# Unread identity products in TensorE's waits, LayerNorm numbers computed a stage ahead, and the gate weights quantised in the first stage

## The chip, the cores and the metric

One core of one Trainium2 chip. A core has TensorE (PE, matrix products, results in PSUM), VectorE (DVE), ScalarE (ACT), GpSimd (POOL) and SyncE (SP, which here only issues transfers). Each engine works through its own list of instructions in order and waits on semaphores for the others. The metric is the device time of one execution in microseconds, the median of three runs.

## The reference, cut to what matters

Four pairs of attention and feed-forward, each on a LayerNorm of a running x of 16 sequences x 128 tokens x 256 features, and each added to x.

```python
x = x + xattn0(_layernorm(x), ctx, ctx)   # autocorrelation by rfft/irfft, top 4 lags
x = x + ffn0(_layernorm(x), w_gate, w_up, w_down)
x = x + xattn1(_layernorm(x), ctx, ctx)   # 16 heads, window of 64
x = x + ffn1(_layernorm(x), slot_embeds, w1, b1, w2, b2)
x = x + xattn2(_layernorm(x), ctx, ctx)   # full attention
x = x + ffn2(_layernorm(x), W_r, W_k, W_v, mu_r, mu_k)
x = x + xattn3(_layernorm(x), ctx, ctx)   # rotary attention
x = x + ffn3(_layernorm(x), W1, b1, W2, b2, Wr, br)   # 8 experts, the best 2 of each token

def ffn0(x, w_gate, w_up, w_down):          # 4-bit weights in blocks of 32, 16-bit activations
    x = act_qdq(x)                          # scale: the maximum over the whole tensor
    up = act_qdq(x @ lpbq_dequant(w_up).T)
    gate = act_qdq(x @ lpbq_dequant(w_gate).T)
    sig = fixed_qdq_u16(jax.nn.sigmoid(gate))
    gate = act_qdq(gate * sig)
    return act_qdq(gate * up) @ lpbq_dequant(w_down).T

def ffn1(x, norm_gamma, slot_norm_gamma, slot_embeds, w1, b1, w2, b2):
    xn, sn = rmsnorm(x, norm_gamma), rmsnorm(slot_embeds, slot_norm_gamma)
    logits = jnp.einsum('bnd,esd->bnes', xn, sn)
    dispatch = jax.nn.softmax(logits, axis=1)
    combine = jax.nn.softmax(logits.reshape(b, n, e * s), axis=-1)
    slots = jnp.einsum('bnd,bnes->besd', xn, dispatch)
    h = jax.nn.gelu(jnp.einsum('besd,edh->besh', slots, w1) + b1)
    eo = (jnp.einsum('besh,ehd->besd', h, w2) + b2).reshape(b, e * s, DIM)
    return jnp.einsum('bmd,bnm->bnd', eo, combine)

def ffn2(x, W_r, W_k, W_v, mu_r, mu_k):     # x_prev: x of the token before
    xr, xk = mu_r * x + (1 - mu_r) * x_prev, mu_k * x + (1 - mu_k) * x_prev
    return sigmoid(xr @ W_r.T) * (square(relu(xk @ W_k.T)) @ W_v.T)
```

## The kernel before

The running x lies in SBUF for the whole program as X[:, n], 16 tiles of 128 tokens x 256 features (B = 16 tiles, G4 = 4 groups of four), and beside it `stats`, the sums that `batch_stats` (L89) takes of each tile once it has been added to. The eight stages run one after the other as functions of their own: autocorrelation (tiles and semaphores named ac_), quantised FFN (qf_), windowed attention (at_), slot FFN (sl_), full attention (at_ again), receptance FFN (rf_), rotary attention (at_), routed FFN (mo_). In the trace they begin at about 0, 122, 327, 498, 1394, 1554, 1623 and 1813 us. Each has a list of instructions for each engine, written out in its order by hand; there is no planner. At a stage's end `Tiles.clear` (L74 to 76) frees the semaphores and makes all engines meet at a barrier. `Early` holds the little that is loaded across it: the identity, the first group's context, the next key weights.

LayerNorm: `layernorm_begin` (L98) turns `stats` of all 16 tiles into mean and 1/sqrt(variance) with 16 aggregates (L102) and a chain of steps on 16 numbers per partition, each waiting for the one before (L104 to 111: add epsilon, an integer first guess, three Newton steps). It stands first in DVE's list in every stage but the first, which does it in two parts (`layernorm_part`, L135); the slot FFN has it written out. Then DVE normalises tile by tile, PE turns each tile with the identity into PSUM, and ACT or DVE copies it out.

Quantised FFN (`quantised_ffn`, L1231): DVE makes the numbers, normalises x tile by tile and takes each tile's maximum (L1544, L1548), with the quantising of the gate weights put in after tile 7 (L1517 to 1525: block maxima, scale, reciprocal, times inverse, rounding, times scale). After the last maximum it makes the scale of the whole tensor, rounds x (L1576), splits it in two halves (L1581), and PE's first hidden products follow (L1386). GATE's results are evicted, rounded by ACT (L1448), put through the sigmoid (L1453), whose table ACT loads just before the first, rounded by POOL (L1333, L1335) and multiplied on DVE (L1591). The UP products are evicted between these. The output products (L1395) wait for `prod_made`.

Attention (`attention`, L507): PE projects keys (L619), values (L653) and queries of each group of four tiles, turns x (L660), in the rotary kind also multiplies by a half-swap matrix (L646, `swap_halves`). Then a loop over the 16 sequences makes maxima (score products L687), their transpose (L694), the scores against keys (L707), the shift (L718) and the weighed values (L730) in a staggered order, and DVE and ACT follow one step behind.

Slot FFN (`slot_ffn`, L2137): 24 rows (8 of x, 8 of the slots, 8 of x) are split by DVE in two f16 halves and turned by PE (`turn_row`, L2264) in one list; then 32 steps of hidden and result products. Receptance FFN (L1026): per group a turn (L1073), products (L1081, L1087) and values (L1096). Routed FFN (L1690): logits of each tile (L1840, L1846) once br has landed, a chain on DVE that picks experts and places rows, gathers by POOL (L1967), and 23 tiles of hidden (L1889) and output products (L1900).

## Time and profile before

| | us |
|---|---|
| median of three runs (2156.86, 2160.91, 2163.70) | 2160.91 |
| profiled execution | 2156.95 |
| its span | 2154.8 |
| PE busy | 1865.7 (87%) |
| DVE busy | 1478.9 (69%) |
| ACT busy | 1116.7 (52%) |
| POOL busy | 157.5 (7%) |
| mean granted clock of TensorE | 0.928 |

A granted clock of 1.00 is 2.4 GHz, one of 0.50 is 1.2 GHz. Busy shares are means over stages with different limits: the slot FFN's 896 us and the routed FFN's 341 us are nearly all PE; the openings are not. The 2.1 us between the span and the execution's time lie around it.

### The profile page before, as it was taken

Reading aid. Unit: us, or ns where it says so; the run is one execution under the profiler, and the core shown is the slowest. Engines: PE = TensorE matmul, PEld = TensorE weight load, DVE = VectorE, ACT = ScalarE, POOL = GpSimd, SP = SyncE. Lnnn points to the kernel's source line nnn. Section 1 sums busy time; section 2 is a strip of 40 time slices with the busy share of each in tenths; the row PEclk is TensorE's granted clock in tenths of the full one; section 3 lists DMA queues with packets and bytes.
Section 4 is the critical chain, followed back from the end, with each engine's and each line's share of the span. In section 5 each row is a group of like instructions: output and inputs, shape, how many; then the busy total and the mean of one; then the engine's idle time right before and its main releaser. Section 6 shows DMA issues by size and latency. Waiting matters only on the chain. (4 is left out here: it accounts for less than half of the span.)

```text
span 2154.8 us, 40850 instructions
## 1 busy us (share of the span) xinstructions
PE 1865.7 (87%) x16258; PEld 1345.9 (62%) x16258; DVE 1478.9 (69%) x3056; ACT 1116.7 (52%) x1888; POOL 157.5 (7%) x122
## 2 busy tenths in 40 slices
PE   7949269894799999999999999889787797499995
PEld 7924145673377666677777666556564476398884
DVE  6677874556777777777777776836556565688886
ACT  3425753445356566665666565344441454367772
POOL 0001300001000000000000000000000000135441
PEclk9969689996999999999999999999988898599998
DMA  4010001002100000000000000000001000477775
GB/s 143 1 50 1 0 1 50 2 2 90 40 21 21 21 27 34 21 21 21 21 20 21 2 1 1 22 29 2 22 0 53 1 2 26 152 238 251 248 249 184
DMA packets 79451, 113.68 MB, mean 53 GB/s; under 512 B 9696, under 2 KB 62624, under 8 KB 79136
## 3 DMA queue, kind: packets, MB, share of 16 engines
q1 hardware_dynamic: 74848, 99.01, 14.1%
q0 software_dynamic: 4416, 12.06, 1.5%
q8 instruction: 131, 2.15, 0.4%
q14 instruction: 56, 0.46, 0.1%
HBM read 100.83 MB, written 10.22 MB: 52 GB/s over the span
## 5 line engine op out<-in xcount | busy, mean ns | idle before, releaser
L2344 PE MATMUL sl_ps_eo<-sl_w,sl_hT 128*128 128x256 f16 x3072 | 353.2, 273 | 0.8 <-DVE sl_hT L2582 0.7
L2321 PE MATMUL sl_ps_h<-sl_slot_inT,sl_w 128*128 128x512 f16 x1536 | 338.7, 380 | 0.5 <-ACT sl_h L2458 0.5
L2344 PEld LDWEIGHTS sl_ps_eo<-sl_w,sl_hT 128*128 128x128 f16 x3072 | 298.4, 98 | 35.9 <-DVE sl_hT L2582 1.3
L2458 ACT ACTIVATE sl_h<-sl_ps_h,sl_b1T 128x512 f32<-128x512 f32 x256 | 175.7, 687 | 170.0 <-PE sl_ps_h L2321 162.9
L2321 PEld LDWEIGHTS sl_ps_h<-sl_slot_inT,sl_w 128*128 128x128 f16 x1536 | 150.4, 98 | 176.3 <-issue 1.4
L2582 DVE TENSOR_TENSOR sl_hT<-sl_h,sl_hT 128x512 f16<-128x512 f32 x256 | 177.0, 692 | 102.1 <-ACT sl_hT L2461 97.8
L950 DVE TENSOR_REDUCE at_neg_max<-at_ps 128x8 bf16<-128x1024 f32 x96 | 117.0, 1221 | 144.2 <-PE at_ps L687 144.2
L1889 PE MATMUL mo_ps_h<-mo_xgT,mo_w 128*128 128x256 f16 x1104 | 128.0, 277 | 5.4 <-issue 4.2
L1900 PE MATMUL mo_ps_eo<-mo_w,mo_hT 128*128 128x256 f16 x1104 | 124.1, 273 | 0.0
L1889 PEld LDWEIGHTS mo_ps_h<-mo_xgT,mo_w 128*128 128x128 f16 x1104 | 109.5, 100 | 20.9 <-issue 6.6
L2593 DVE SCALAR_TENSOR_TENSOR sl_result<-sl_ps_eo,sl_b 128x256 f32<-128x256 f32 x128 | 54.3, 424 | 97.6 <-PE sl_ps_eo L2344 93.3
L1900 PEld LDWEIGHTS mo_ps_eo<-mo_w,mo_hT 128*128 128x128 f16 x1104 | 107.2, 98 | 12.0
L845 ACT ACTIVATE at_probT<-at_ps 128x1024 f32<-128x1024 f32 x96 | 98.6, 1027 | 25.5 <-PE at_ps L718 25.5
L1949 ACT ACTIVATE mo_h<-mo_ps_h,mo_b 128x256 f32<-128x256 f32 x184 | 77.0, 475 | 54.0 <-issue 46.6
L1008 POOL MEMSET at_v<- 128x2048 f32 x6 | 10.7, 1817 | 1150.5 <-POOLq L76 1150.5
L852 ACT ACTIVATE at_attT<-at_ps 128x256 f32<-128x256 f32 x48 | 18.4, 383 | 140.5 <-PE at_ps L744 140.5
L1967 POOL DMA_INDIRECT mo_xg<-x_rows,mo_from_i x46 | 66.2, 1440 | 247.7 <-DVE mo_from_i L2057 233.5
L2461 ACT ACTIVATE sl_hT<-sl_h 128x512 f16<-128x512 f32 x128 | 80.6, 629 | 4.0
L1395 PE MATMUL qf_ps_out<-qf_w_outT,qf_prodT 128*128 128x256 f16 x288 | 34.1, 279 | 49.2 <-DVE qf_prodT L1608 46.1
L1386 PE MATMUL qf_ps<-qf_xqT,qf_w_inT 128*128 128x512 f16 x288 | 66.9, 393 | 9.8 <-DVE qf_xqT L1581 6.7
L2437 ACT ACTIVATE sl_combT<-sl_ps_lt 128x512 f32<-128x512 f32 x32 | 19.1, 597 | 108.4 <-PE sl_ps_lt L2300 108.4
L2075 DVE SCALAR_TENSOR_TENSOR mo_w<-mo_w_raw,mo_w 128x1024 f16<-128x1024 f32 x46 | 56.2, 1223 | 17.4 <-issue 9.0
(385 smaller groups left out, 3631.1 us busy)
## 6 DMA issues: line engine op xcount, KB each, us to landing
mo_w_raw<-in_L_ffn_W SPq DMA_DIRECT2D x46, 1024.0 KB, 7.4
sl_w_in<-in_L_ffn_w SPq DMA_DIRECT2D x16, 1024.0 KB, 5.3
at_ctxT<-ctxT SPq DMA_DIRECT2D x9, 512.0 KB, 6.9
mo_w_raw<-pair_rows SPq DMA_DIRECT2D x4, 1024.0 KB, 9.0
mo_b<-in_L_ffn_b SPq DMA_DIRECT2D x23, 128.0 KB
at_wT<-L_attention_w SPq DMA_DIRECT2D x9, 256.0 KB, 7.0
ac_ctx_all<-in_ctx SPq DMA_DIRECT2D x4, 512.0 KB, 7.3
x_rows<-mo_xrow SPq DMA_DIRECT2D x4, 512.0 KB, 2.9
```

Of the source, the lines that this page charges most:

```text
L845: act.activation(probT[:, n % 2, 2 * pair:2 * pair + 2].rearrange("p r j q -> p r (j q)"), ps[:, at:at + 2], ACT.Exp, scale=SCALE).then_in ...
L950: dve.tensor_reduce(neg_max[:, 2 * pair:2 * pair + 2, 0:HR], ps[:, at:at + 2].rearrange("p r (j k) -> p r j k", j=HR), AX.X, ALU.max, nega ...
L1386: last = pe.matmul(pair(q)[:, g], w_inT[:, w, i, k, c * P:(c + 1) * P], xqT[:, x, k, tokens], start=(k, a) == (0, 0), stop=(k, a) == (C - ...
L1889: last = pe.matmul(ps_h[:, q % 3, j % 2], w1_of(m, wp)[:, k, j * P:(j + 1) * P], xgT[:, m % 2, xp, k], start=(k, a) == (0, 0), stop=(k, a) ...
L1900: last = pe.matmul(ps_eo[:, s, 0:D], hT[:, m % 2, hp, j, s * P:(s + 1) * P], w2_of(m, wp)[:, j], start=(j, a) == (0, 0), stop=(j, a) == (H ...
L1949: act.activation(h[:, q % 2, j % 2], ps_h[:, q % 3, j % 2], ACT.Relu, bias=b1[:, m % WB, j:j + 1], scale=1.0 / W_SCALE).then_inc(h_ready, 1)
L1967: pool.indirect_dma_start(xg[:, m % XB, s], None, env.x_rows, bass.IndirectOffsetOnAxis(ap=from_i[:, q:q + 1].bitcast(U32), axis=0)).then_ ...
L2321: last = pe.matmul(ps_h[:, j % 2], w1[:, e % 2, w, k, j * P:(j + 1) * P], slot_inT[:, q % 2, x, k].rearrange("p b s -> p (b s)"), start=(k ...
L2344: last = pe.matmul(ps_eo[:, b % 2, 0:D], hT[:, hp, j, b * P:(b + 1) * P], w2[:, e % 2, w, j], start=(j, a) == (0, 0), stop=(j, a) == (HJ - ...
L2458: act.activation(h[:, j % 2], ps_h[:, j % 2], ACT.Gelu, bias=b1T[:, q // G4, j:j + 1], scale=1.0 / W_SCALE).then_inc(h_ready, 1)
L2461: act.activation(hT[:, 0, j], h[:, j % 2], ACT.Copy).then_inc(h_high, 1)
L2582: dve.tensor_tensor(hT[:, 1, j], h[:, j % 2], hT[:, 0, j], ALU.subtract).then_inc(h_split, 1)
```

## The change

`hold_clock` multiplies the identity by itself into a PSUM bank that nothing reads at that time, so many times. It is called in PE's list at these places: quantised FFN, 18 after the sixth product has been made and before the outputs, 3 at the end; every attention, 3 (rotary: 10) before the last two queries are waited for (rotary: the last plain ones), 4 before the scores of steps 0 and 1, 2 in step 1, 3 at the end, and in the rotary kind 3 in each of the four groups between the swap and the values; slot FFN, 8 first, one before each row from m = 4, 12 at the end; receptance FFN, 5 first, 8 after turn(1), 10 before the last values, 8 at the end; routed FFN, 6 before turn_x(0), 16 before turn(0), 8 before hidden(1).

The mean and the 1/sqrt of tiles 0 to 11 for the quantised, slot, receptance and routed FFN are computed near the end of the stage before (`normal_ahead`, once `stats` of 12 tiles are restated); tiles 12 to 15 follow in the stage itself (`normal_rest`). The results lie in tiles that outlive the stages (`env.ahead`). The attentions keep `layernorm_begin`.

The gate weights are loaded in the first stage, behind wo on SP's queue and ahead of the context of groups 1 to 3, and quantised in place in four pieces by DVE after pairs 2 to 5. In the quantised FFN x is rounded and split in two halves of two groups, a spare sigmoid of one column stands before the wait for x, the first two UP evictions come after the second sigmoid, and five instead of four UP roundings come before the silus.

```diff
+def hold_clock(pe, env, bank, count):
+
+    ident = env.early.ident
+    for _ in range(count):
+        pe.matmul(bank, ident[:], ident[:], start=True, stop=True)
...
+AHEAD = 12
+
+
+def normal_ahead(dve, t, env, nth, stats_known, value, rows_only=False):
+
+    env.ahead.rows_only = rows_only
+    dve.wait_ge(stats_known, value)
+    layernorm_part(dve, t, env.ahead, nth, 0, AHEAD)
+
+
+def normal_rest(dve, t, env):
+
+    layernorm_part(dve, t, env.ahead, 0, AHEAD, B)
...
             load_weight(wo, "wo", wo_in)
+            env.gate_weights.load(sp)
             for g in range(1, G4):
...
+                if 2 <= j < 6:
+                    env.gate_weights.quantise(dve, j - 2)
+            normal_ahead(dve, t, env, 2, restated, AHEAD)
             add_pair(NPAIRS - 1)
...
                 if rotary:
                     swap_halves(C * g)
+                    enough(pe, xT_ready, 4 * g - 1)
+                    hold_clock(pe, env, ps[:, 6, 0:P], 3)
...
+            if rotary:
+                pe.wait_ge(plain_ready, 2 * JOBS - 1)
+            else:
+                pe.wait_ge(proj_out, 2 * JOBS - C)
+            hold_clock(pe, env, ps[:, 0, 0:P], 10 if rotary else 3)
             pe.wait_ge(proj_out, 2 * JOBS)
             pe.wait_ge(w_in[WO], 16)
             for n in range(B + 3):
                 if n < B:
                     turn_maxima(n)
+                if n == 1:
+                    hold_clock(pe, env, ps[:, 6, 0:P], 2)
...
                     output(n - 3)
+                if n < 2:
+                    hold_clock(pe, env, ps[:, 6, 0:P], 4)
...
+            hold_clock(pe, env, ps[:, 0, 0:P], 3)
...
+                if n == AHEAD + 3:
+                    normal_ahead(dve, t, env, 1, restated, AHEAD, rows_only=windowed)
                 if n >= 3:
                     restate(n - 3)
...
+            hold_clock(pe, env, ps_r[:, 0, 0:P], 5)
             turn(0)
             turn(1)
+            hold_clock(pe, env, ps_r[:, 0, 0:P], 8)
             pe.wait_ge(weights_in, 48)
...
+            hold_clock(pe, env, ps_x[:, 0, 0], 10)
             value(G4 - 1)
+            hold_clock(pe, env, ps_x[:, 0, 0], 8)
...
+            normal_group(0)
             dve.memset(xT[:, :, :, :, 0:1], 0.0).then_inc(zeroed, 1)
-            layernorm_begin(dve, t)
-            normal_group(0)
...
             mix(1)
+            normal_rest(dve, t, env)
             key(0)
...
-UP_OUT = (((0,), (1,)), ((2,), (3,)), ((4, 5), ()), ((6, 7), ()), ((8, 9), ()), ((10, 11), ()))
+UP_OUT = (((), (0, 1)), ((2,), (3,)), ((4, 5), ()), ((6, 7), ()), ((8, 9), ()), ((10, 11), ()))
...
+            pe.wait_ge(prod_made, FC)
+            hold_clock(pe, env, ps[:, 0, 0:P], 18)
             for n in range(B):
                 output(n)
+            hold_clock(pe, env, ps[:, 0, 0:P], 3)
...
+            act.activation(spare_sig[:], constant[:, 1:2], ACT.Sigmoid).then_inc(table_loaded, 1)
             act.wait_ge(x_ready, G4)
...
-            layernorm_begin(dve, t)
             for n in range(B):
                 normal_x(n)
...
-                if n == 7:
-                    for piece in range(4):
-                        quantise_weights(0, piece)
-                if n == 11:
-                    weights_low(0)
+                if n == AHEAD - 1:
+                    weights_low_tile(0)
+                    weights_low_tile(1)
+                    normal_rest(dve, t, env)
+                    weights_low_tile(2)
...
-            for g in range(G4):
-                round_x(g)
-            for g in range(G4):
-                low_x(g)
+            for half in range(2):
+                for g in (2 * half, 2 * half + 1):
+                    round_x(g)
+                for g in (2 * half, 2 * half + 1):
+                    low_x(g)
...
+            hold_clock(pe, env, ps_h[:, 0, 0, 0:P], 6)
             turn_x(0)
...
             pe.wait_ge(table_ready, 1)
+            hold_clock(pe, env, ps_h[:, 0, 0, 0:P], 16)
             turn(0)
             for m in range(NTILES):
+                if m == 1:
+                    hold_clock(pe, env, ps_eo[:, 0, 0:P], 8)
                 hidden(m)
...
-            layernorm_begin(dve, t)
             for n in range(B):
+                if n == AHEAD:
+                    normal_rest(dve, t, env)
...
+            hold_clock(pe, env, ps_eo[:, 1, 0:P], 8)
             pe.wait_ge(consts_in, CONSTS)
...
             for m in range(NT):
+                if m >= 4:
+                    hold_clock(pe, env, ps_eo[:, 1, 0:P], 1)
                 turn_row(m)
...
             combine(STEPS - 1, 3)
+            hold_clock(pe, env, ps_h[:, 0, 0:P], 12)
...
+                if m == FIRST_SLOT + E + AHEAD - B // 2 - 2:
+                    normal_rest(dve, t, env)
                 if FIRST_SLOT <= m < NT - 2:
                     row(m + 2)
```

## Rows read from the trace of the kernel before

**Rows 1.** Line of the page: TensorE's granted clock in tenths, 40 slices
```profile
PEclk9969689996999999999999999999988898599998
```

**Rows 2.** The table of stretches: us, each engine's busy time, granted clock, DMA share, GB/s
```profile
1812.80:1874.20 61.40, 28.74 (x174) 26.32 (x175) 36.45 (x157) 15.61 (x39) 8.60 (x8) 0.50 0.47 148
...
600.00:1390.00 790.00, 786.63 (x5976) 550.28 (x5974) 575.35 (x1164) 470.00 (x848) 0.00 (x0) 1.00 0.05 17
```

**Rows 3.** The same table, PE alone: two runs of one-tile f32 products
```profile
9.96:13.51 3.55, 3.55 (x16) 1.00 1.11 355
...
18.45:20.23 1.78, 1.78 (x17) 1.00 1.07 369
```

**Rows 4.** Timeline (start, us, engine, line, tiles, [idle before <- releaser]): DVE, first stage
```profile
48.45 0.87 DVE L436 MAX8 ac_top<-ac_corr 128x8 f32<-128x128 f32 x4 [2.03 <-ACT ac_corr L378]
...
120.08 0.69 DVE L463 TENSOR_TENSOR X<-X,ac_ps_out 128x512 f32<-128x512 f32 x1 [6.52 <-PE ac_ps_out L324]
```

**Rows 5.** Timeline, DVE and PE, opening of the quantised FFN
```profile
122.88 1.17 DVE L102 BATCH_NORM_AGGREGATE qf_meanvar<-stats 128x2 f32<-128x6 f32 x16
...
126.60 0.73 DVE L1544 TENSOR_SCALAR qf_xn_ring<-X,qf_meanvar,qf_rstd 128x256 f32<-128x256 f32 x2
...
131.47 1.74 DVE L1517 TENSOR_REDUCE qf_wmax<-qf_upT 128x48 f32<-128x1536 f32 x1
...
136.75 1.76 DVE L1525 TENSOR_TENSOR qf_upT<-qf_upT,qf_wscale 128x1536 f32<-128x1536 f32 x1
...
153.98 5.25 PE L1386 MATMUL qf_ps<-qf_xqT,qf_w_inT 128*128 128x512 f16 x16 [6.67 <-DVE qf_xqT L1581]
```

**Rows 6.** Timeline, ACT, the first sigmoid
```profile
200.18 1.28 ACT L1453 ACT_TABLE_LOAD   x1
```

**Rows 7.** Timeline, PE, output products of the quantised FFN
```profile
287.55 5.50 PE L1395 MATMUL qf_ps_out<-qf_w_outT,qf_prodT 128*128 128x256 f16 x36 [46.10 <-DVE qf_prodT L1608]
...
293.50 4.09 PE L1395 MATMUL qf_ps_out<-qf_w_outT,qf_prodT 128*128 128x256 f16 x36 [0.45 <-DVE stats L91]
```

**Rows 8.** Timeline, POOL, opening of the slot FFN
```profile
507.04 4.61 POOL L2509 MEMSET sl_acc<- 128x4112 f32 x1 [8.22 <-ACT sl_acc L2414]
```

**Rows 9.** Timeline, PE, first keys of the full attention
```profile
1394.66 6.21 PE L619 MATMUL at_ps<-early_ctxT,early_wk 128*128 128x512 f32 x8 [5.01 <-PEq L76]
...
1400.70 3.60 PE L619 MATMUL at_ps<-at_ctxT,early_wk 128*128 128x512 f32 x8
```

**Rows 10.** Timeline, PE, first steps of the full attention
```profile
1454.56 2.09 PE L687 MATMUL at_ps<-at_KT,at_QT 32*128 32x128 f32 x32 [0.99 <-ACT at_probT L845]
...
1462.01 1.17 PE L687 MATMUL at_ps<-at_KT,at_QT 32*128 32x128 f32 x32
```

**Rows 11.** Timeline, DVE and PE, receptance FFN
```profile
1563.75 2.74 DVE L1161 SCALAR_TENSOR_TENSOR rf_mixedT<-rf_xT,rf_mu_rest,rf_now 128x512 f32<-128x512 f32 x4 [3.30 <-ACT rf_now L1122]
...
1565.31 6.22 PE L1081 MATMUL rf_ps_r<-rf_wT,rf_mixedT 128*128 128x256 f32 x16 [0.96 <-DVE rf_mixedT L1161]
...
1604.12 3.62 PE L1096 MATMUL rf_ps_v<-rf_wT,rf_keyT 128*128 128x256 f32 x16
...
1612.23 6.66 PE L1096 MATMUL rf_ps_v<-rf_wT,rf_keyT 128*128 128x256 f32 x16 [4.49 <-DVE rf_keyT L1169]
```

**Rows 12.** Timeline, DVE and PE, rotary attention
```profile
1647.04 0.69 DVE L924 TENSOR_TENSOR at_by_sin<-at_ps,at_sinT 128x512 f32<-128x512 f32 x1 [0.57 <-PE at_ps L646]
...
1706.36 0.29 PE L694 MATMUL at_ps<-at_ident_b,at_neg_max 128*128 128x128 bf16 x1 [4.42 <-ACT at_QT L825]
```

**Rows 13.** Timeline, PE, routed FFN's opening
```profile
1818.74 1.11 PE L1840 MATMUL mo_ps_t<-mo_ident,mo_xn_all 128*128 128x128 f32 x4 [7.59 <-DMA mo_br<-in_L_ffn_br]
...
1836.48 1.72 PE L1846 MATMUL mo_ps_m<-mo_wr,mo_xT 128*128 128x8 f32 x8
...
1869.92 7.49 PE L1889 MATMUL mo_ps_h<-mo_xgT,mo_w 128*128 128x256 f16 x48 [1.21 <-ACT mo_xgT L1926]
...
1880.96 7.07 PE L1889 MATMUL mo_ps_h<-mo_xgT,mo_w 128*128 128x256 f16 x48 [3.11 <-issue]
```

More of the change, by code:

```diff
@@ L1271, in quantised_ffn @@
         spare = upT[:].rearrange("p c n -> p (c n)").rearrange("p (s n) -> p s n", n=FF * C)
[L1272 removed]
+        raw, raw_t = [spare[:, 0], env.gate_weights.raw[:], spare[:, 6]], [spare[:, 2], None, spare[:, 7]]
         x_ints = xT[:].bitcast(I16).rearrange("p c (n half) -> p c n half", half=2)[:, :, :, 0]
@@ L1494, in _ @@
                     weights_high_tile((6, 8)[c])
-            for c in range(4):
+            for c in range(UP_FIRST):
                 round_up(c)
@@ L2720, in __init__ @@
         self.x_rows, self.pair_rows = scratch
-        self.early = None
+        self.early = self.ahead = self.gate_weights = None
+class Ahead:
+    def __init__(self, nc, ctx):
+        self.meanvar = ctx.enter_context(nc.sbuf_tensor("ahead_meanvar", [P, B, 2], F32))
+        self.rstd = ctx.enter_context(nc.sbuf_tensor("ahead_rstd", [P, B, 1], F32))
+        self.rows_only = False
 class Early:
@@ L2762, in build_program @@
         env.early = Early(nc, ctx, env)
-        for phase in PHASES:
+        env.ahead = Ahead(nc, ctx)
+        with ExitStack() as first:
+            env.gate_weights = GateWeights(nc, first, env)
+            for phase in PHASES[:2]:
+                phase(nc, env)
+        for phase in PHASES[2:]:
             phase(nc, env)
```

146 lines of the change are left out of this document (83 added, 63 removed).

## The prediction, made before the changed kernel was run

> **What bounds the kernel now.** I read the page's table of busy shares and its line of granted clock first [rows 1]. TensorE is busy for 87% of the span, but the clock line has digits under 9: there the engine runs at 1.2 GHz instead of 2.4. The table of stretches shows both kinds of time [rows 2]: from 600 to 1390 us (the slot FFN's steps) PE is busy 786.63 of 790 us at full clock, and nothing the change does can shorten that. From 1812.8 to 1874.2 it is busy 28.74 of 61.4 us at a granted clock of 0.50, while it waits for others. The same view, laid over every digit under 9, gives half-clock stretches of some 310 us in all, all at openings, ends and first steps of stages; much of them is idle PE, where the clock costs nothing.
>
> Each stage closes with a barrier of all engines (L74 to 76), so a microsecond gained in a stage's opening moves everything behind it. The sum is therefore made stage by stage: for each edit I ask what the last wait of that stretch was. The chain of waits only shows the last stage, so I used the timelines of the stretches around the edits.
>
> **The price of a hold.** One hold is one 128x128 f32 product. The forward transforms of the first stage have this form: eight of them (16 records) take 3.55 us at the slow pace and 1.78 us, with a 17th record at the edge, at the fast one [rows 3]; the clock column says 1.00 for both, as it has no record yet for the first, so it is the pace that tells them apart. So a hold is about 0.43 us at half clock and 0.222 us at full. The change issues 189 of them: 84 us if all stood on the path at the slow price, 0 if all fall into waits.
>
> **Part 1: first stage (autocorrelation).** The load of w_gate goes onto SP's queue ahead of the context of groups 1 to 3. Its 786 KB delay them by an estimated 2 to 4 us, and the second group's context is there 9 us before PE first wants it: nothing. The four pieces of quantising it (6.95 us in all, in rows 5 from 131.47 to 138.42, pieces of 2.49, 1.79, 1.00 and 1.67) go to DVE after pair j = 2 to 5; DVE waits 2.03 us for the correlation ahead of its top-values step [rows 4]. Only the first piece is longer, by 0.46, and PE has more slack than that. Cover gone, they would cost up to 7 us. The LayerNorm numbers of tiles 0 to 11 (full chain 3.7 us, below, less 4 of 16 aggregates: 3.4 us) go into DVE's idle 6.52 us before the last pair [rows 4]. All of part 1: 0.
>
> **Part 2: quantised FFN.** DVE runs this opening: PE waits 6.67 us until 153.98 for the split activations [rows 5]. The LayerNorm chain starts at 122.88 and the first normalised row comes at 126.60, 3.7 us later; the quantising takes 131.47 to 138.42, 6.95 us. Both go; normal_rest (4 tiles: 0.3 us of aggregates plus the same 2.5 us of small dependent steps, 2.8) comes in; the memsets (0.3) move behind the first row. 3.7 + 6.95 + 0.3 - 2.8 = 8.2, and 0.5 of a wait for weights_low that the early gate weights shorten: 8.7. Rounding in two halves lets the first product start two round_x earlier less one low_x, which the rows give as 1.4 - 0.5 of wait: 0.8. Sum +9.5 (bounds 8 to 10.5; below nothing is excluded, since DVE's list before that product only gets shorter).
> The sigmoid's table load of 1.28 us stands on ACT's path to the first silu [rows 6]; a spare sigmoid ahead, in a wait of ACT, takes it out, and the two evictions that no longer stand before the second sigmoid give 0.4 more: +1.7 (bounds 0 to 2.2, as POOL's rounding passes between sigmoid and silu can collide with DVE). The Trainium skill (ScalarE: Activation LUTs, What ACT_TABLE_LOAD costs) prices a change of table at 2.66 us with its drain; by it the sum would be 1.4 better, but here the next activation starts 0.02 us after the load, so the row's 1.28 stands.
> 18 holds wait for the sixth product and stand in the 8 us before the output products: 4.0 us warm, 7.7 cold. The first output pair took 5.50 us, the next 4.09 [rows 7]: +1.3 (bounds -0.5 to 1.4).
>
> **Part 3: windowed attention.** Three holds at the end of the stage before are free (DVE still works), and the first keys get faster, but the next transfer's landing then binds: +0.6. The holds of its middle fit into waits, where the clock is full anyway: 0. Its own LayerNorm chain remains. The early numbers for the slot FFN (3.4 us) go into a DVE wait of 3.8 us in its tail: 0.
>
> **Part 4: slot FFN.** Taking the chain out of the opening buys little: POOL's clearing of the accumulator, which comes after the constants have landed, runs from 507.04 to 511.65 [rows 8], and DVE's split behind it waits: +0.2. normal_rest now sits in DVE's row list before row 20, where PE waits for rows: -0.8. A hold before each of the 20 rows from m = 4: between 0 and 20 x 0.43 = 8.6, but most rows have a PE wait of 0.2 to 2.7 us in front; I take 0.4. The 8 in the opening are free. Sum -1.0 (bounds +1.5 to -5).
> 12 holds at its end lie beside DVE's last adds; the full attention's first keys took 6.21 us, the next eight products 3.60 [rows 9]. The second half waits for ctxT, which leaves 1.0; at two in three: +0.7 (0 to 2.6).
>
> **Part 5: full attention.** Its first steps run at half clock: the row of 32 score products takes 2.09 us, and 1.17 where the clock is full [rows 10]. Three large groups there are slow (two of L707, one of L687, 0.9 each), and the small ones between them add 0.6: +3.3 (bounds 0 to 4). It needs the 3 + 4 + 4 + 2 holds to lie in the waits of 0.99 to 1.5 us there; four warm holds are 0.9 us, four cold ones 1.7.
>
> **Part 6: receptance FFN.** The chain of 3.7 us [rows 5] stands before everything: DVE's mix waits 3.30 us for ACT at 1563.75 and the receptance products start at 1565.31 at half clock with 6.22 us [rows 11]. The constants land before ACT would want them: +3.7. The 8 holds behind turn(1) cost 1.8 warm or 3.4 cold in a wait of at most 3.8, and make the first products up to 2.6 faster: +0.5 (bounds -2.5 to 2.6). The last value group took 6.66 us after a wait of 4.49, the one before 3.62 [rows 11]: 10 holds in that wait: 3.0 x 0.73 = +2.2.
>
> **Part 7: rotary attention.** DVE keeps its LayerNorm here and runs the groups. Three holds per group stand before the values. DVE waits there for PE's swap products (0.57 us) and for values [rows 12]: 4 x 3 holds cost 0.2 + 3 x 0.67 = 2.2 at the warm price; they avoid two slow spells worth 2.7: +0.5 (bounds -2.2 to 2.7). In the middle PE waits 4.42 us for the last queries, then makes both first steps at half clock [rows 12]. Ten warm holds are 2.2 us and fit. Four large groups at 0.92 each less what the first transfer of clock costs: +3.4 (0 to 4.2).
>
> **Part 8: routed FFN.** PE's first instruction waits 7.59 us for br's transfer [rows 13], so the absent LayerNorm gives nothing; the 6 holds come behind that wait and before turn_x(0), and the rows of logits follow, 16 from 1818.74 to 1838.2, PE-bound at 1.17 us each [rows 13]: 6 x 0.43 = -2.6 (bounds -2.6 to +5, the latter if the clock rises: ACT needs 0.8 us a row). 16 holds lie between the table and the first gathered rows, 8 us: free, 6.9 cold. Then hidden(0) takes 7.49 us and hidden(1) 7.07 [rows 13], while a warm one is 5.24. ACT's list binds between them, so 2.0 + 1.8 = 3.8, at 0.8: +3.1. Sum +0.5.
>
> **The sum.** 9.5 + 1.7 + 1.3 + 0.6 - 1.0 + 0.7 + 3.3 + 3.7 + 0.5 + 2.2 + 0.5 + 3.4 + 0.5 = 26.9. The profiled execution took 2156.95: 2130.0. The median of the three runs shown is 4 us higher (2160.91, from 2156.86 to 2163.7), so I add half of that: **2132 us**.
>
> **The rivals.**
> **A, the forecast:** most spots stay at full clock. 0.62, range 2123 to 2140.
> **B, the clock falls as before.** Small products do not keep it up where the rest of the stretch is transposes or idle, and the openings with many transposes stay at 0.50. For it: the slot opening, the receptance turns and the logits rows are busy at half clock already and did not rise [rows 2, 11, 13]. Then only DVE's and ACT's parts pay, 9.5 + 1.7 + 3.7 = 14.9, less some 4 us of cold holds on the path: 2146, with the same 2 us 2148. 0.15. The Trainium skill (TensorE: Matmul & The Clock Gate, Part 4) says that a transpose doesn't count as busy for the gate as a matmul does; that would be this case, and the half clock in the logits rows agrees with it.
> **C, it stays up everywhere,** also through the slot FFN's rows and the logits: 2.6 given back and 5.0 gained in the logits, 0.8 in the last values, 0.7 in the hidden ones, 1.9 in the keys, 1.0 in the slot rows: 12.0 off A, 2120. 0.15.
> **D, slower: holds in front of waited-for work.** PE takes its list in order; in the row list of the slot FFN (20), the rotary groups (12), the receptance opening (13), the routed opening (6) and the first steps of the attentions (30) a hold that outlives its wait delays the next product by 0.43 us. These 81 cost 34.8 if none is covered. DVE's gains of 14.9 to 15.5 are eaten from 36 uncovered holds on; with 66 the time is 2156.95 + 28.4 - 15.5 = 2170. Against it: most stand before a wait of 1 us or more. 0.04.
> **E, the work laid into waits collides:** the quantising and four early chains delay their stages by some 14 us, and the time stays within 0.3%: 0.04.
>
> **How the numbers follow.** Time 2132. The range 2116 to 2148 takes in the centres of B and C and leaves out D, E and the outer parts. A measurement here tells about 0.3%, 6.5 us, from no change. Faster 0.62 + 0.15 + 0.14 of B = 0.91; same 0.05 (E, the rest of B); slower 0.04.
>
> **What would show it.** In the changed profile: first product of the quantised FFN near 144.5 and no fall of DVE at its start; granted clock 1.0 at the first steps of the two later attentions (score rows of 1.17 us), at the last values (3.62), at hidden(0) and hidden(1) (5.24 each); the logits rows still 1.17 apart and 2.6 later; the slot FFN's first hidden product up to 1 us later counted from its barrier. Wrong it is if the holds appear as idle PE shortened but the clock line does not move (B), or if the DVE rows after a hold show a longer wait for PE than before (D).

## The result, and the profile after

The changed kernel took 2126.63 us (median of four, 2124.36 to 2135.47), the kernel before on the same chip 2160.16; the ratio is 0.9852, 95% interval 0.982 to 0.9884. The forecast was 2132, range 2116 to 2148. The same kernel was run again beside two groups of experiments: 2130.2 (ratio 0.9867, 0.9847 to 0.9886) and 2134.89 (0.9869, 0.985 to 0.9888). Its 13 executions on record lie between 2124.36 and 2136.13 (mean 2130.8), the 35 of the kernel before between 2155.59 and 2165.27 (mean 2160.4), and the profile was taken of the slowest of the first four, 2135.47. So the first profile shows 21.5 us of gain where the medians show 33.5, and I read it with care: three profiles of the changed kernel stand in the tables below.

The page of the changed kernel, its busy line and the line of granted clock (tenths, 40 slices). They answer [rows 1]:

```profile
PE 1893.7 (89%) x16636; PEld 1385.7 (65%) x16636; DVE 1485.9 (70%) x3105; ACT 1117.0 (52%) x1889; POOL 154.9 (7%) x122
...
PEclk9979589997999999999999999999999998699997
```

The 378 records more on PE are the 189 unread products. The digits under 9 in the last third are fewer, those at the left end and before the end are not. The mean granted clock rose from 0.928 to 0.951, 0.957 and 0.953 in the three profiles (0.932 with the moves alone, 0.946 with the holds alone).

Lengths of the stages, from one stage's last semaphore clearing to the next one's, in us, read from the traces of the changed kernel's three profiles (2135.47, 2127.8 and 2135.07 us).

| stage | before | changed, first | changed, second | changed, third | forecast gain | gain in the three |
|---|---|---|---|---|---|---|
| autocorrelation | 122.2 | 124.0 | 124.2 | 124.1 | 0 | -1.8, -2.0, -1.9 |
| quantised FFN | 204.3 | 194.7 | 193.6 | 193.1 | 12.5 | 9.6, 10.7, 11.2 |
| windowed attention | 170.9 | 170.6 | 170.6 | 170.6 | 0.6 | 0.3, 0.3, 0.3 |
| slot FFN | 896.8 | 895.7 | 895.0 | 896.9 | -1.0 | 1.1, 1.8, -0.1 |
| full attention | 159.5 | 155.2 | 155.4 | 154.8 | 4.0 | 4.3, 4.0, 4.7 |
| receptance FFN | 69.0 | 60.5 | 58.9 | 60.6 | 6.4 | 8.5, 10.1, 8.4 |
| rotary attention | 190.1 | 188.4 | 186.8 | 188.6 | 3.9 | 1.7, 3.3, 1.5 |
| routed FFN | 341.5 | 343.9 | 340.9 | 344.0 | 0.5 | -2.4, 0.6, -2.5 |
| sum | 2154.2 | 2133.0 | 2125.4 | 2132.6 | 26.9 | 21.2, 28.8, 21.6 |

The lines that answer the groups of before, from the timeline of the changed kernel (start, us, engine, line, tiles, idle before and its releaser). The opening of the quantised FFN; the stage starts 1.84 us later than before:

```profile
145.73 1.86 PE L1471 MATMUL qf_ps<-qf_xqT,qf_w_inT 128*128 128x512 f16 x4 [5.97 <-DVE qf_xqT L1670]
```

The first hidden product comes at 145.73 instead of 153.98 [rows 5]; counted from the stage's start that is 10.1 us earlier. The full attention's first steps, answering [rows 10]:

```profile
1443.54 1.17 PE L756 MATMUL at_ps<-at_KT,at_QT 32*128 32x128 f32 x32 [0.38 <-ACT at_probT L926]
...
1446.14 1.15 PE L776 MATMUL at_ps<-at_QT,at_KT 32*128 32x256 f32 x16 [0.34 <-DVE at_neg_max L1031]
```

Both large groups are at full clock (before: 2.09 each, at 1454.56 and 1458.08). The receptance FFN, answering [rows 11]:

```profile
1545.35 1.95 PE L53 MATMUL rf_ps_r<-early_ident 128*128 128x128 f32 x16
...
1547.35 2.83 PE L1164 MATMUL rf_ps_r<-rf_wT,rf_mixedT 128*128 128x256 f32 x12
...
1591.74 5.32 PE L1179 MATMUL rf_ps_v<-rf_wT,rf_keyT 128*128 128x256 f32 x16 [2.26 <-DVE rf_keyT L1256]
```

The eight holds take 1.95 us and the receptance products come behind them at full clock; the last values took 5.32 here, so the clock fell inside them (before 6.66), and 3.72 in the second profile. The routed FFN's opening, answering [rows 13]:

```profile
1794.86 2.93 PE L53 MATMUL mo_ps_h<-early_ident 128*128 128x128 f32 x12 [6.60 <-DMA mo_br<-in_L_ffn_br]
...
1797.58 1.06 PE L1930 MATMUL mo_ps_t<-mo_ident,mo_xn_all 128*128 128x128 f32 x4
...
1846.94 0.62 PE L1967 MATMUL mo_ps_t<-mo_ident_h,mo_xg 128*128 128x128 f16 x8 [1.89 <-DMA mo_xg<-x_rows,mo_from_i]
...
1848.76 8.15 PE L1980 MATMUL mo_ps_h<-mo_xgT,mo_w 128*128 128x256 f16 x48 [1.21 <-issue]
...
1860.22 3.98 PE L1980 MATMUL mo_ps_h<-mo_xgT,mo_w 128*128 128x256 f16 x35 [1.02 <-issue]
```

Six holds run for 2.72 us at half clock after br has landed, and the first transposes follow them. The 16 holds before the gathered rows ended 1.89 us too early, and hidden(0) took 8.15 (before 7.49; 7.07 and 6.80 in the second and third profile). The last row shows 35 of the 48 products of hidden(1), which took 5.40 in all, at full clock, behind 8 holds of its own.

### The profile page after: what moved, and what is told of

The parts are those of the page before. It is cut to its first block and busy times, and to the rows that moved or that the text cites. A ratio compares the mean times of both kernels' runs of the same rounds, so it can differ in the third digit from the quotient of the medians.

```text
span 2133.6 us, 41665 instructions
## 1 busy us (share of the span) xinstructions
PE 1893.7 (89%) x16636; PEld 1385.7 (65%) x16636; DVE 1485.9 (70%) x3105; ACT 1117.0 (52%) x1889; POOL 154.9 (7%) x122
## 5 line engine op out<-in xcount | busy, mean ns | idle before, releaser
L1991 PE MATMUL mo_ps_eo<-mo_w,mo_hT 128*128 128x256 f16 x1104 | 124.1, 273 | 0.0
L1091 POOL MEMSET at_v<- 128x2048 f32 x6 | 10.7, 1817 | 1138.4 <-POOLq L83 1138.4
L2164 DVE TENSOR_TENSOR mo_hT<-mo_h,mo_hT 128x512 f16<-128x512 f32 x92 | 63.8, 694 | 3.2
```

Of the source, the lines that this page charges most:

```text
L1991: last = pe.matmul(ps_eo[:, s, 0:D], hT[:, m % 2, hp, j, s * P:(s + 1) * P], w2_of(m, wp)[:, j], start=(j, a) == (0, 0), stop=(j, a) == (H ...
L2164: dve.tensor_tensor(hT[:, m % 2, 1, 2 * p:2 * p + 2], h[:, q % 2], hT[:, m % 2, 0, 2 * p:2 * p + 2], ALU.subtract).then_inc(h_split, 1)
```

## The experiments

All edits are to the changed kernel, unless it says otherwise.

**Each half alone.** The edit of the first: `range(0)` in `hold_clock`. The second is the kernel before with all calls of `hold_clock`.

```diff
     for _ in range(count):
+    for _ in range(0):
```

> The changed kernel with its 189 unread products left out and everything else of the change in (LayerNorm numbers ahead, gate weights early, spare sigmoid, halves). Theory 1 (the gains are of two kinds, some 15 us of DVE's lists in the quantised and receptance openings and the rest TensorE's clock): the quantised FFN stays about 10 us shorter, the receptance FFN 3.7 shorter, the full attention as before (159.5), the routed FFN as before (341.5); time near 2146, a gain of 13 to 15. Theory 2 (holds cost about as much as they give): the time is within 3 us of the changed kernel.

Measured: 2148.92 us (ratio 0.9941, 0.9924 to 0.9957).

> The kernel before with all 189 unread products and nothing else of the change. Theory 1: the full attention 4.3 us shorter, the receptance FFN 3 to 5 shorter, the rotary attention 1.7 shorter, the routed FFN 2.4 longer where its logits stay at half clock; time near 2148. If gains simply add, its gain and that of the kernel without the products sum to the 33 us measured for both. Theory 2: the time is within 3 us of the kernel before.

Measured: 2149.11 us (ratio 0.9939, 0.992 to 0.9959).

Each half is worth about 13 us, and both together 26 to 33 by the medians, 28 to 32 by the ratios. Whether they add exactly can't be told from the times. By stages (us gained over the kernel before, from the profiles):

| stage | moves alone | holds alone | both (three profiles) |
|---|---|---|---|
| quantised FFN | 8.0 | 1.9 | 9.6 to 11.2 |
| slot FFN | -2.5 | 1.3 | -0.1 to 1.8 |
| full attention | -0.8 | 4.2 | 4.0 to 4.7 |
| receptance FFN | 4.8 | 2.0 | 8.4 to 10.1 |
| rotary attention | 1.1 | 1.7 | 1.5 to 3.3 |
| routed FFN | -5.7 | -2.6 | -2.5 to 0.6 |

Theory 1 holds for the kinds of gain: full attention from the clock alone, quantised opening from DVE's list alone (its first hidden product comes 21.7 us into the stage with the moves alone, 31.8 with the holds alone and before). Two stage forecasts missed: the routed FFN wasn't as before but 5.7 longer with the moves alone, and the receptance FFN gained 2.0 instead of 3 to 5 with the holds alone. That stage gains more from both than the sum of 6.8, and the table of stretches shows why. It gives 10.2 us of its opening with the moves alone, with the holds alone and with both, the last from the second profile; they begin 1.1, 3.3 and 2.4 us into the stage (span, then busy time of PE, PEld, DVE, ACT and POOL with instructions, granted clock, DMA share, GB/s):

```profile
1549.80:1560.00 10.20, 7.23 (x24) 5.87 (x25) 7.03 (x19) 7.31 (x11) 0.00 (x0) 0.51 0.33 103
```

```profile
1550.70:1560.90 10.20, 6.64 (x30) 6.27 (x31) 6.77 (x20) 5.78 (x9) 0.00 (x0) 0.50 0.23 66
```

```profile
1541.20:1551.40 10.20, 8.86 (x50) 7.01 (x49) 8.00 (x20) 9.46 (x13) 0.00 (x0) 1.00 0.30 96
```

Only with both is the granted clock 1.00; over exactly the first 10.2 us of the stage it is 0.57, 0.66 and 1.00 (and 1.00 in the first profile too). With the holds alone PE first stands idle for DVE's LayerNorm chain, the clock falls, and the eight holds behind the turns go at the slow price:

```profile
1552.96 1.97 PE L1092 MATMUL rf_ps_x<-early_ident,rf_xn_groups 128*128 128x128 f32 x8 [3.83 <-DVE rf_xn_groups L1175]
...
1557.96 3.36 PE L53 MATMUL rf_ps_r<-early_ident 128*128 128x128 f32 x16
...
1561.15 3.62 PE L1100 MATMUL rf_ps_r<-rf_wT,rf_mixedT 128*128 128x256 f32 x16
```

The first receptance products then start 2.0 us later than before, at full clock. With the early numbers that idle time is gone and the same eight take 1.95 us.
The routed FFN's -5.7 is for the most part something else. In its loop over 23 tiles PE waits now and then:

```profile
1950.48 0.71 PE L1980 MATMUL mo_ps_h<-mo_xgT,mo_w 128*128 128x256 f16 x5 [1.63 <-issue]
```

Such waits sum to 5.65 us in this profile, to 1.1 in that of before and to 2.0, 2.6 and 2.7 in the three of the changed kernel. Here PE waits for ACT's copy of the gathered rows, which ends at 1950.38. It stands in ACT's list behind the roundings of the weights, and those began only after ACT had stood idle for 3.22 us:

```profile
1943.39 1.06 ACT L2025 ACTIVATE mo_w<-mo_w_raw 128x1024 f16<-128x1024 f32 x1 [3.22 <-issue]
...
1949.33 1.05 ACT L2020 ACTIVATE mo_xgT<-mo_ps_t 128x1024 f16<-128x1024 f16 x1
```

Two tiles earlier the trace names the weights' transfer as what ended such an idle time of ACT (1.51 us), so I call these waits late weights; for this one the releaser isn't shown. They differ between executions of one kernel, and no edit here touches that loop.

**The changed kernel again,** unchanged.

> The changed kernel once more, unchanged, for a second profile. Its profiled execution took 2135.47 and the three others 2124.36 to 2127.31. Theory A (the difference is whether the clock rises during the routed FFN's logits): in a profile of about 2126 the logits rows come under 1 us apart instead of 1.17 and the routed FFN is 5 to 8 us shorter than 343.9. Theory B (it is spread over many spots): no stage differs by over 3 us between the two profiles.

Measured: 2130.2 (2127.8 to 2136.13), profiled execution 2127.8. The rows of the logits in this profile:

```profile
1790.76 2.34 PE L53 MATMUL mo_ps_h<-early_ident 128*128 128x128 f32 x10
...
1792.90 1.06 PE L1930 MATMUL mo_ps_t<-mo_ident,mo_xn_all 128*128 128x128 f32 x4
...
1794.58 0.41 PE L1930 MATMUL mo_ps_t<-mo_ident,mo_xn_all 128*128 128x128 f32 x2
...
1796.55 0.42 PE L1930 MATMUL mo_ps_t<-mo_ident,mo_xn_all 128*128 128x128 f32 x2
...
1797.54 0.73 PE L1936 MATMUL mo_ps_m<-mo_wr,mo_xT 128*128 128x8 f32 x4
...
1798.13 0.67 PE L1930 MATMUL mo_ps_t<-mo_ident,mo_xn_all 128*128 128x128 f32 x2
...
1799.30 0.67 PE L1930 MATMUL mo_ps_t<-mo_ident,mo_xn_all 128*128 128x128 f32 x2
```

The rows 1794.58 to 1797.54 are at full clock, 0.62 to 0.74 apart, the later ones 1.17 apart again. The holds cost 2.4 us here too and this spell gives 2.6 back. So theory A has the right place, but less than half of the difference of 7.7 us between the two profiles: routed FFN 3.0 (A wanted 5 to 8), receptance 1.6, rotary 1.6, quantised 1.1, slot 0.8. Theory B's bound of 3 us holds. It is spread.

**Without the 6 holds before the logits.**

```diff
-            hold_clock(pe, env, ps_h[:, 0, 0, 0:P], 6)
             turn_x(0)
```

> The changed kernel without the 6 products ahead of the routed FFN's first transposes. If these 6 only cost their 2.6 us at half clock, the routed FFN takes 341.3 and the median is 2 to 3 us under the changed kernel's. If they are what lifts the clock for the logits in most executions, it is 3 to 6 us slower than the changed kernel and its logits rows come 1.17 us apart.

Measured: 2130.76 (ratio 0.9862, 0.9843 to 0.988), no difference from the changed kernel that can be told. The routed FFN took 342.72 with its logits at half clock throughout, between the two states it has with the holds (340.9 and 344.0). Neither outcome that I had written down came: with one profile of each state, the six look like a bet that comes out even.

**What eats the sigmoid's table load.** The table load is off the path in the changed kernel:

```profile
184.41 1.28 ACT L1571 ACT_TABLE_LOAD   x1
...
188.25 2.10 ACT L1536 ACTIVATE qf_gateT<-qf_gateT,qf_constant,qf_inv 128x2048 f32<-128x2048 f32 x1 [2.35 <-DVE qf_inv L1659]
...
190.38 2.00 ACT L1541 ACTIVATE qf_xT<-qf_gateT,qf_scale 128x2048 f32<-128x2048 int16 x1
```

but POOL's first rounding starts 2.2 us after the sigmoid's end at 192.38, and 7.04 after the reduction over partitions, with no releaser:

```profile
187.22 0.35 POOL L1414 PARTITION_ALL_REDUCE qf_all_max<-qf_own_max  x1 [46.63 <-DVE qf_own_max L1649]
...
194.61 1.89 POOL L1418 TENSOR_SCALAR qf_xT<-qf_xT 128x2048 f32<-128x2048 f32 x1 [7.04 <-issue]
```

In the kernel before it started 7.11 after the reduction too, and then that looked like waiting for the sigmoid (203.48):

```profile
196.13 0.35 POOL L1329 PARTITION_ALL_REDUCE qf_all_max<-qf_own_max  x1 [48.06 <-DVE qf_own_max L1560]
...
203.58 1.89 POOL L1333 TENSOR_SCALAR qf_xT<-qf_xT 128x2048 f32<-128x2048 f32 x1 [7.11 <-ACT qf_xT L1453]
```

The edit puts a one-column operation between.

```diff
             combine_maxima(GS)
+            pool.wait_ge(max_all, GS + 1)
+            pool.tensor_scalar(spare_pool[:], all_max[:, GS:GS + 1], 1.0, 0.0, ALU.min, ALU.max).then_inc(pool_spare, 1)
             for c in range(FC):
```

> The changed kernel with one POOL operation on a single column right behind the second reduction over partitions, before the sigmoids are rounded. In four profiles with the early table load POOL's first rounding starts 6.8 to 7.4 us after that reduction ends and about 2 us after the sigmoid is there. Theory 1 (POOL needs these 7 us before any ordinary operation, whatever it waits for): the small operation starts about 7 us after the reduction and the first rounding still comes 2 us after the sigmoid; time unchanged, near 2128. Theory 2 (something with the sigmoid or with DVE's reductions delays the rounding): the small operation runs at once, and the rounding either still comes 2 us late (DVE) or follows the sigmoid within 0.2 us, which makes the stage about 2 us shorter.

```profile
185.89 0.35 POOL L1416 PARTITION_ALL_REDUCE qf_all_max<-qf_own_max  x1 [46.55 <-DVE qf_own_max L1653]
...
192.99 0.18 POOL L1426 TENSOR_SCALAR qf_spare_pool<-qf_all_max 128x1 f32<-128x1 f32 x1 [6.75 <-issue]
...
193.25 1.89 POOL L1420 TENSOR_SCALAR qf_xT<-qf_xT 128x2048 f32<-128x2048 f32 x1
```

Measured: 2128.38 (0.9835 to 0.9876). Theory 1: the operation waits for nothing but the reduction, whose result DVE already uses 0.03 us after its end, and starts 6.75 us after that end. POOL didn't start other work sooner in any of the fourteen profiles (6.59 to 7.52 us), and the table load of before lay beside that. The list of transfers has, between the reduction and the next POOL operation, one packet of the instruction queue (here of the changed kernel; one in the kernel before too, 0.3%):

```profile
q14 instruction: 1, 0.01, 0.4%
```

That POOL loads code in this time is what this suggests; it isn't shown, as that queue has 57 packets in the whole program, many of them while POOL stands idle. The Trainium skill (GPSIMD Engine Reference, 2.1 Instruction dispatch) says that the first call of a freshly loaded kernel costs some 6 us with no instruction in the profile; the 6.59 to 7.52 us of fourteen profiles are of that size, though the page's load follows another instruction and this one a reduction.

**Without the rotary groups' holds.**

```diff
-                    enough(pe, xT_ready, 4 * g - 1)
-                    hold_clock(pe, env, ps[:, 6, 0:P], 3)
```

> The changed kernel without the three unread products in each of the four rotary groups. Theory 1 (each group's products lie on the path PE to DVE and cost 0.67 us; the clock would fall in one or two groups without them): opening shorter by 2.7 less 1 to 2.7 of slow spells, so the rotary attention takes 186.5 to 188.5 against 188.4 and 186.8 in the two profiles of the changed kernel. Theory 2 (they pay): it takes 189 to 190.

Measured: 2135.04 (ratio 0.9884, 0.9861 to 0.9907), the rotary attention 193.05, more than before the change (190.07).

```profile
1604.85 3.36 PE L722 MATMUL at_ps<-at_wT,early_ctxT 128*128 128x256 f32 x8
...
1608.01 1.28 PE L715 MATMUL at_ps<-at_plain,at_half_swap 128*128 128x512 f32 x2
...
1611.22 3.07 PE L722 MATMUL at_ps<-at_wT,early_ctxT 128*128 128x256 f32 x8 [1.94 <-DVE at_v L1022]
```

Three of the first five rows of values take 3.1 to 3.4 us, against 1.9 at full clock, and the granted clock is at half in six stretches of the stage instead of one to three. A group's three holds take the 0.67 us that I gave them. Neither theory named a time as long as this, and that the holds pay isn't shown. The other two kernels without them reach the first transposed maxima sooner, 82.1 us (moves alone) and 83.8 us (before) into the stage against 90.0 here, and those with them need 84.8 to 89.5. The interval of the ratio overlaps the changed kernel's.

**Without the slot rows' holds.**

```diff
-                if m >= 4:
-                    hold_clock(pe, env, ps_eo[:, 1, 0:P], 1)
```

> The changed kernel without the 20 single products before the slot FFN's rows. Theory 1 (they fall into PE's waits and keep the clock up in parts of the opening): the slot FFN gets longer, toward the 899.3 of the kernel without any products, from 895.7 and 895.0. Theory 2 (rows are bound by DVE, the clock is worth little there): it stays within 0.7 us of 895.4.

Measured: 2134.49 (ratio 0.9895, 0.9869 to 0.9922), slot FFN 896.65, against 895.0 to 896.9 with them. That is 1.2 above the 895.4 of theory 2 and far from the 899.3 of theory 1; they are worth nothing that can be told. The routed FFN took 345.57 in its profile, with 3.45 us of late weights.

**Longer runs of holds.**

```diff
-            hold_clock(pe, env, ps[:, 0, 0:P], 18)
+            hold_clock(pe, env, ps[:, 0, 0:P], 30)
-            hold_clock(pe, env, ps_h[:, 0, 0, 0:P], 6)
-            hold_clock(pe, env, ps_h[:, 0, 0, 0:P], 16)
+            hold_clock(pe, env, ps_h[:, 0, 0, 0:P], 24)
```

> The changed kernel without the 6 products before the logits, with 30 instead of 18 before the quantised FFN's outputs and 24 instead of 16 before the routed FFN's first gathered rows. In the profile of the changed kernel PE stands idle 2.95 us between the 18 and the outputs and 1.9 to 2.7 us between the 16 and the rows, and in both places the first real products are at half clock again. Theory 1 (it is this gap that lets the clock fall): the first output pair takes 4.1 instead of 5.5 us and the first hidden products 5.4 instead of 7.1 to 8.2; quantised FFN 1.4, routed FFN 1.5 to 2.5 shorter, and 2 from the 6 left out. Theory 2 (the products don't hold the clock at these places at all): both stay slow, and the longer run before the outputs starts them later by up to 1 us.

The quantised outputs in the first profile of the changed kernel, and with 30 holds:

```profile
270.73 5.86 PE L53 MATMUL qf_ps<-early_ident 128*128 128x128 f32 x36 [37.29 <-DVE qf_gateT L1689]
...
279.54 7.74 PE L1480 MATMUL qf_ps_out<-qf_w_outT,qf_prodT 128*128 128x256 f16 x54 [2.95 <-DVE qf_prodT L1697]
```

```profile
269.03 9.34 PE L53 MATMUL qf_ps<-early_ident 128*128 128x128 f32 x60 [37.30 <-DVE qf_gateT L1689]
...
278.21 4.09 PE L1480 MATMUL qf_ps_out<-qf_w_outT,qf_prodT 128*128 128x256 f16 x36
```

Thirty holds reach up to the outputs, which run at full clock, and put them off by 0.4 us. But with 18 the first pair was fast too in six of the eight profiles of kernels with the moves and 18 holds: from its start to the next pair's they take 4.55 us, the two others 5.61 and the kernel before 5.95; from its start to the stage's end 37.5 to 37.6, 39.2 and 38.9. So this is worth 1.3 us in two executions of eight and costs 0.4 in the rest. Before the gathered rows theory 1 failed. The 24 holds end 0.44 us before the transposes of the rows, and hidden(0) takes 7.07 us all the same, not 5.4; PE then still waits 1.95 us for ACT's copy, and the granted clock falls within the first 0.9 us of hidden(0):

```profile
1840.89 0.62 PE L1966 MATMUL mo_ps_t<-mo_ident_h,mo_xg 128*128 128x128 f16 x8 [0.44 <-DMA mo_xg<-x_rows,mo_from_i]
...
1843.46 7.07 PE L1979 MATMUL mo_ps_h<-mo_xgT,mo_w 128*128 128x256 f16 x48 [1.95 <-ACT mo_xgT L2019]
```

Measured: 2130.61 (0.9849 to 0.9903). No difference that can be told.

**All products relaid.** 24 holds ahead of the wait for br in place of 6 behind it, 24 before the slot FFN's constants, 14 at the receptance FFN's end, 30 and 24 as above. The part of the edit that isn't a mere count, beside the 6 that go:

```diff
         @block.tensor
         def _(pe):
+            hold_clock(pe, env, ps_h[:, 0, 0, 0:P], 24)
             pe.wait_ge(consts_in, CONSTS)
```

> The changed kernel with its unread products laid out by what the profiles showed: 30 instead of 18 before the quantised outputs, 24 instead of 16 before the routed FFN's gathered rows, 24 ahead of the wait for br in place of the 6 behind it, 24 instead of 8 ahead of the slot FFN's constants, 14 instead of 8 at the end of the receptance FFN. Theory 1 (a product in front of the wait costs nothing and keeps the clock up for what follows): the routed FFN's first transposes come at 6 us of the stage as in the kernel before instead of 8.4, at least the first rows of logits at full clock; routed FFN 337 to 340, slot FFN 0 to 1 shorter, time 2 to 5 us under the control's. Theory 2 (24 products outlive the wait because the clock falls in them): first transposes at 8 us or later, no gain.

```profile
1797.77 1.06 PE L53 MATMUL mo_ps_h<-early_ident 128*128 128x128 f32 x8
...
1798.66 0.60 PE L1931 MATMUL mo_ps_t<-mo_ident,mo_xn_all 128*128 128x128 f32 x4
...
1799.99 0.41 PE L1931 MATMUL mo_ps_t<-mo_ident,mo_xn_all 128*128 128x128 f32 x2
...
1805.41 0.42 PE L1931 MATMUL mo_ps_t<-mo_ident,mo_xn_all 128*128 128x128 f32 x2
```

Measured: 2130.67 (ratio 0.9861, 0.9846 to 0.9876). The routed FFN took 336.5, 4.4 to 7.4 less than the changed kernel's: the rows of logits are 0.6 to 0.75 apart for 8 us, and the first transposes come 5.8 us into the stage, as in the kernel before. But the rotary attention took 192.4, and the time can't be told from the control's (0.9869).

**The routed FFN's alone.** To see whether that was luck, the changed kernel with only the 24 ahead of the wait for br in place of the 6, and 24 instead of 16 before the gathered rows:

> The changed kernel with only the routed FFN's products laid out anew: 24 ahead of the wait for br in place of 6 behind it, 24 instead of 16 before the gathered rows. Theory 1 (the 4 to 7 us that the routed FFN gained in the run with all relayed products are real, and the rotary attention's 192.4 there was a matter of when its slow spells fell, not of this edit): routed FFN 336 to 338, the stages before it in the range of the changed kernel's four profiles (rotary 186.8 to 188.6), ratio to the kernel before 0.982 to 0.985, against 0.985 to 0.987 of the changed kernel. Theory 2: the routed FFN is again 341 or more.

Measured: 2130.17 (ratio 0.9858, 0.9837 to 0.9879). Routed FFN 340.1, rotary attention 192.56, with the same four slow spells as in the run before (from about 9, 29, 57 and 91 us of the stage). All three figures of theory 1 missed (336 to 338, 186.8 to 188.6, 0.982 to 0.985). The rotary attention's code is untouched, and spells at these times came in the run without the group holds too; that the edit has no part in them is argued from this, not shown, since both kernels with it took 192.4 or more. The smaller gain has a cause that shows. The 24 holds end 5.9 us into the stage in both runs, but here br had not landed by then:

```profile
1790.82 5.60 PE L53 MATMUL mo_ps_h<-early_ident 128*128 128x128 f32 x48 [1.22 <-PEq L83]
...
1797.66 0.66 PE L1931 MATMUL mo_ps_t<-mo_ident,mo_xn_all 128*128 128x128 f32 x4 [1.24 <-DMA mo_br<-in_L_ffn_br]
```

The transposes began 7.2 us into the stage instead of 5.8, and the clock fell at 11.2 instead of 14.0. No version beats the changed kernel by what can be measured.

**Every hold twice.**

```diff
-    for _ in range(count):
+    for _ in range(2 * count):
```

> The changed kernel with every unread product issued twice, 378 instead of 189. Theory 1 (most of them fall into waits; only those of the rotary groups, the slot rows, and the routed opening stand on the path): rotary attention 12 x 0.22 = 2.7 longer, routed opening up to 2.6 longer, slot opening 1 to 4 longer, the other stages within 1 us; time 2134 to 2138. Theory 2 (the clock gained so far was not complete): the first steps and openings gain more than this and the time is under the control's. The slower case of the prediction (uncovered products at 0.43 us each) would give 189 x 0.43 = 81 us more.

Measured: 2142.82 (ratio 0.9915, 0.99 to 0.993), 8 us more than the control beside it by the medians and 10 by the ratios. By stages against the three profiles: slot FFN +3 to +5, rotary +2.6 to +4.4, full attention +1.5 to 2.2, windowed +1.3, receptance +1 to 2.6, routed -2.3 to +0.7. Theory 1, but above its 2134 to 2138, with more places on the path than I listed: the attentions' first steps too. In one place doubling did what 16 and 24 holds had not: the holds reach the transposes of the gathered rows, and hidden(0) runs at full clock:

```profile
1846.95 9.26 PE L53 MATMUL mo_ps_h<-early_ident 128*128 128x128 f32 x64 [1.21 <-DVE mo_from_i L2152]
...
1857.88 5.40 PE L1980 MATMUL mo_ps_h<-mo_xgT,mo_w 128*128 128x256 f16 x48 [1.22 <-ACT mo_xgT L2020]
```

> The changed kernel unchanged, on the same chip as the two beside it: 2126 to 2131.

Measured: 2134.89 (2124.36 to 2135.08).

## Why the prediction was right, and where its terms were not

**Direction and size** are right: 2132 against 2126.63, 2130.2 and 2134.89. The case that came is A. Against B: with the moves alone the gain is 13, so it is the clock that makes up the other half. C came nowhere in full: each profile has 13 to 16 stretches at half clock, 185 to 211 us in all, against 19 and 311 before. D did not come: even 378 holds leave the kernel 18 us faster than before. E came in no stage; the pieces in DVE's waits cost nothing that shows.

**Quantised opening, +9.5:** 10.1. The step held: DVE's list was the bound and got shorter by what was taken out.

**Table load, +1.7:** -0.4 to 0.5. This term failed. The path from the first gate rounding on ACT to the first silu was 10.33 us before and 9.82 to 10.74 in the twelve profiles with the early table load. I bounded it by collisions of POOL and DVE, and they exist: the third silu takes 2.3 us in four of the twelve and 3.4 to 3.95 in eight, and 2.3 before.

```profile
212.84 1.90 POOL L1418 TENSOR_SCALAR qf_sig_more<-qf_sig_more 128x2048 f32<-128x2048 f32 x1 [1.06 <-ACT qf_sig_more L1541]
...
213.01 3.87 DVE L1680 SCALAR_TENSOR_TENSOR qf_gateT<-qf_sig_more,qf_gateT 128x2048 f32<-128x2048 f32 x1
```

This is a loss of 1.1 to 1.7 us that I had bounded and not counted. The fourth silu took 3.99 before and 3.4 in all twelve, which gives 0.6 back. The stage as a whole gained 12.6 to 13.2 us in the four (forecast 12.5) and 8.0 to 11.2 in the eight. But on the path to the first silu the mechanism was another: a second thing, POOL's 6.6 to 7.5 us behind the reduction, ended at about the same time as the sigmoid (203.1 to 204.0 by that range, and 203.48).

**Output products, +1.3:** 1.4 in six of eight profiles. In the two others, the first profile among them, the first pair gained 0.3, and up to the stage's end they lost 0.3.

**Autocorrelation, 0:** -1.8 to -2.0 in three profiles, but 122.3 with the moves alone and 121.7 in the run without logit holds, against the 122.2 of before. The kernel before with holds only has this stage unchanged and took 123.8, so this is not the change's cost. In the first profile 1.5 of it lies where the fast pace began later at the start:

```profile
14.78 3.58 PE L342 MATMUL ac_ps_q<-ac_wq,ac_specT 128*128 128x256 f32 x8 [1.21 <-ACT ac_specT L426]
```

This group took 1.97 before and nothing of the change comes ahead of it but a transfer's issue. Quantising itself cost what was forecast: the wait of 2.03 us shrank to 1.23, 1.07 and 0.43 and in the first piece to none.

**Windowed attention, +0.6:** 0.3.

**Slot FFN, -1.0:** between -0.1 and 1.8. I took normal_rest and the single holds for losses. The single holds are near nothing; with the moves alone the stage was 2.5 us longer and with the holds alone 1.3 shorter, in one profile each, and what of the moves costs this was not separated.

**Full attention, +4.0:** 4.0 to 4.7, by the mechanism given: 3.4 to 3.5 behind the first transposed maxima (forecast 3.3), 0.6 to 1.3 ahead of them (0.7).

**Receptance, +6.4:** 8.4 to 10.1. The chain gave the 3.7 of the forecast, as the moves alone show. The first receptance products at full clock (3.7 instead of 6.2) and the turns at half the time were taken at 0.5 for both; they gave 3.4 in all three profiles, since the holds fitted into the wait. The last values gave 1.2 to 2.9 (2.2).

**Rotary, +3.9:** 1.5 to 3.3. From the first transposed maxima on the stage gained 3.3, 4.5 and 3.2 (forecast 3.4). Up to there it lost 1.6, 1.2 and 1.7 against the kernel before, where I had +0.5 for the groups: their holds cost 2.7 at the warm price and slow spells still come.

**Routed FFN, +0.5:** the 6 holds cost 2.4 (forecast 2.6), hidden(1) gained 1.67 (1.8), hidden(0) between -0.7 and 0.7 (2.0). Its holds end 1.9 to 3.2 us before the rows arrive, and the clock is down again when it runs. This is the step "free, 6.9 cold": I reckoned that they fit, and not when they end; in the first profile they took 6.5, and the clock rose only 0.8 us before the last. Nor is the end of the holds all of it, as the run with 24 shows: the wait for ACT's copy behind the transposes counts too. Only the doubled holds kept the clock.

**The sum, 26.9:** 21.2, 28.8 and 21.6 by the three profiles, all against the one of before, 2156.95, which is near its fastest (median 2160.16). All 13 executions of the changed kernel have a mean of 2130.8. What the table load, the rotary groups and hidden(0) did not give, the receptance and the slot FFN gave beyond their terms; the total was nearer than its parts. That these misses cancel is luck. Three small sums in the working are off by rounding and carry nothing: 189 holds at 0.43 us are 81 us and not 84, 1.4 - 0.5 is 0.9 and not 0.8, and 0.8 of 3.8 is 3.0 and not 3.1.

## What to carry to other kernels

Work that keeps a clock up pays best if it ends when the awaited thing arrives. Holds behind a wait cost their full time (2.4 us for the six before the logits). Holds that end 2 to 3 us early may leave the next products at half clock: hidden(0) in all three profiles, the quantised outputs in two of eight. Holds ahead of a wait that they nearly fill are free (the 24 ahead of br). Moving a LayerNorm chain out of an opening pays where DVE's list is the last thing there (the quantised and the receptance FFN) and nothing where a transfer is (slot and routed FFN). Before a wait is taken off a path, ask of every engine that stood idle beside it since when it could have started; the profile names only the last releaser.

## What the runs showed of the hardware

POOL started no other operation for 6.59 to 7.52 us after the second reduction over partitions in any of the fourteen profiles. In the one with the probe it waited for nothing else.

The spread of the changed kernel's executions (2124 to 2136) goes with slow spells that come or don't come at the same code: the rotary attention took 186.8 us with one, 187.0 to 188.8 with two, 187.9 to 189.7 with three, 192.4 and 192.6 with four (in kernels that have its code unchanged) and 193.05 with six (without the groups' holds). What decides in which execution they come was not settled. Nor was it why PE's waits in the routed loop sum to between 1 and 6 us. The Trainium skill (TensorE: Matmul & The Clock Gate, Part 4) says transposes don't count for the clock as products do. The rows of logits, half of them transposes, let it fall 11.2 to 14.0 us into the stage even when they began at full clock and PE was busy for 7.75 of 8.00 us, which agrees. The slot rows regained it in the middle of their list, for 6.8 us and more with one hold each, and for 3.4 in the kernel before and in the one without these holds; what sets them apart from the logits was not separated.
